# Windowed attention before a mixture of experts: token tiles handled one by one, against groups of four with 32-row score tiles and spare matmuls

## The reference

```python
qkv = layernorm(x) @ W_qkv + b_qkv                # 8 heads of 8 channels
q, k = rope2(q), rope2(k)                         # rotary, by place in an 8x8 window
attn = softmax(q * 8 ** -0.5 @ k.T + mask)        # 64 x 64 for each window and head
x = x + roll(unwindow(attn @ v)) @ W_proj + b_proj
t = layernorm(x)
gates = top2(softmax(t @ router_w.T)), normalized  # 8 experts
x = x + sum_e gates[e] * (silu(t @ w1[e].T) * (t @ w3[e].T)) @ w2[e].T   # 682 hidden
```

## Time and profile before

| | |
|---|---|
| median of 3 runs | 797.75 us (797.47 to 798.89) |
| the profiled execution's own time | 797.36 us |
| its span in the trace | 795.2 us |
| busy: PE, DVE, POOL, ACT | 688.0, 596.1, 514.5, 393.4 us |
| mean granted TensorE clock | 0.905 of full |

### The profile page before, as it was taken

The page is one execution under the profiler, slowest core; times in us unless marked ns, Lnnn a source line. Parts: engine busy times, 40 slices in busy tenths (PEclk is TensorE's granted clock), DMA queues, the critical chain, the costliest instruction groups (busy, mean ns, idle before and its releaser), DMA issues. The chain is left out here.

```text
span 795.2 us, 20947 instructions
## 1 busy us (share of the span) xinstructions
PE 688.0 (87%) x4891; PEld 449.3 (56%) x4891; DVE 596.1 (75%) x2019; ACT 393.4 (49%) x1024; POOL 514.5 (65%) x524
## 2 busy tenths in 40 slices
PE   2998898988898988898610999999999999999992
PEld 2776776766676666676410555555555555555551
DVE  4799969998999988899540577777777777777773
ACT  1455535555555555455311455555555555555551
POOL 3123666777677766665677377767677676767776
PEclk9999859898989989899655899999999999999997
DMA  9400000000000000000013244444344443444442
GB/s 340 169 8 9 22 21 13 17 19 20 20 20 20 22 19 17 20 18 24 23 27 72 39 45 46 45 46 45 44 46 45 46 45 44 45 46 45 45 45 15
DMA packets 83983, 34.17 MB, mean 43 GB/s; under 512 B 80427, under 2 KB 80876, under 8 KB 83436
## 3 DMA queue, kind: packets, MB, share of 16 engines
q0 software_dynamic: 27504, 10.10, 13.9%
q1 hardware_dynamic: 56444, 23.67, 11.6%
HBM read 20.19 MB, written 13.34 MB: 42 GB/s over the span
## 5 line engine op out<-in xcount | busy, mean ns | idle before, releaser
L1071 POOL DMA_INDIRECT out<-y_out,token x159 | 248.1, 1560 | 111.5 <-DVE y_out L955 77.1
L1011 POOL DMA_INDIRECT expert_rows<-rows,slot_u x144 | 147.8, 1026 | 55.2 <-issue 35.4
L502 PE MATMUL bank<-xs,w_sb 64*128 64x384 f32 x510 | 179.9, 497 | 1.4 <-ACT xs L630 0.8
L503 PE MATMUL bank<-xs,w_sb 64*128 64x384 f32 x510 | 180.2, 497 | 0.0
L973 DVE TENSOR_TENSOR hid<-gate_h,bank 128x384 f32<-128x384 f32 x255 | 141.0, 554 | 39.4 <-ACT gate_h L641 22.0
L641 ACT ACTIVATE gate_h<-bank 128x384 f32<-128x384 f32 x255 | 125.4, 492 | 53.7 <-PE bank L503 53.7
L502 PEld LDWEIGHTS bank<-xs,w_sb 64*128 64x128 f32 x510 | 92.1, 188 | 84.1 <-issue 34.8
L516 PE MATMUL bank<-hid,w_sb 128*64 128x384 f32 x612 | 110.0, 494 | 0.0
L503 PEld LDWEIGHTS bank<-xs,w_sb 64*128 64x128 f32 x510 | 92.1, 188 | 0.0
L399 PE MATMUL bank<-k_bd,qkt 128*128 128x512 f32 x144 | 91.3, 722 | 0.0
L650 ACT ACTIVATE y_odd<-bank 64x384 f32<-64x384 f32 x51 | 24.9, 487 | 101.0 <-PE bank L516 101.0
(11 more groups left out here) (129 smaller groups left out, 1330.9 us busy)
## 6 DMA issues: line engine op xcount, KB each, us to landing
xin<-expert_rows SPq DMA_DIRECT2D x51, 99.0 KB
xin<-expert_rows SPq DMA_DIRECT2D x51, 96.0 KB
w_sb<-w SPq DMA_DIRECT2D x1, 3072.0 KB, 22.3
out<-y_out,token POOLq DMA_INDIRECT x159, 3.1
out<-res_all SPq DMA_DIRECT2D x18, 128.0 KB
expert_rows<-rows,slot_u POOLq DMA_INDIRECT x144
x_all<-x_win SPq DMA_DIRECT2D x1, 1664.0 KB, 8.9
res_all<-x_res SPq DMA_DIRECT2D x1, 1664.0 KB, 12.4
```

Of the source, the lines that this page charges most:

```text
L502: pe.matmul(ps_h[c % RING], w13_sb[0:C, e, c, :], xs[0:C, :], start=True, stop=True)
L503: pe.matmul(ps_g[c % RING], w13_sb[C:2 * C, e, c, :], xs[C:2 * C, :], start=True, stop=True).then_inc(s_h, 1)
L1011: pool.indirect_dma_start(rows_dram, bass.IndirectOffsetOnAxis(ap=slot_u[:, i // 2, i % 2:i % 2 + 1], axis=0), rows[:, i // 2, i % 2, :], ...
L1071: pool.indirect_dma_start(out, bass.IndirectOffsetOnAxis(ap=token[:, c:c + 1], axis=0), y_out[:, c, :], None, compute_op=ALU.add).then_inc ...
```

## The change

The attention is now done group by group.

- **Projections are transposed.** ACT writes the normalized tile twice side by side (`xn[P, G, 2, C]`), so that the turned group `xt` holds the same 64 channels in rows 0 to 63 and 64 to 127. Two matmuls with 64 rows and 512 columns give q and k of the whole group, already with channels in rows and with the twin channels beside them. The rotation is one DVE instruction each for q and k (`rotate`), a third matmul with `sum_twins` adds the twins of k, and two ACT copies with a scale by row (`parity`) make `k_bd`. `rope`, `qk_bd`, the turning of q and k, and DVE's `k_bd` are gone.
- **Scores are 32-row tiles.** For a group 64 matmuls of 32 rows, 64 stationary columns and 128 moving columns take the place of four matmuls of 128x512.
- **Work by group.** The turning of `xn` and `att`, the projection, the division, and the residual addition are made for four tiles at once. v is made by 16 matmuls of 64x64.
- **Scaling moves.** Both norms' scaling goes from POOL to ACT (`normalize1`, `normalize2`, four instructions each).
- **Spare matmuls.** `turn_probs` issues two bf16 matmuls of 512 columns ahead of the turning of the last tile's probabilities and six ahead of the first tile's, into `ps_pt`, the bank that the turning overwrites. Nothing reads them.
- The bias of v is folded into that of the projection once.

```diff
+            def head_rows(pair_no, part, fresh):
+                for k in range(2):
+                    for x in range(2):
+                        heads = slice((2 * part + x) * 32, (2 * part + x + 1) * 32)
                         for w in range(2):
+                            toks = slice((2 * pair_no + k) * P + w * N, (2 * pair_no + k) * P + (w + 1) * N)
+                            at = (2 * k + part) * P
+                            mm = pe.matmul(ps[2 * pair_no + x][w * N:(w + 1) * N, at:at + P],
+                                           q_st[heads, toks], k_bd[heads, :, toks], start=fresh, stop=fresh or (part, k) == (1, 1))
...
+            def turn_probs(t, jt, spare=0):
+                after(pe, s_ptc, t, 1)
+                hold(pe)
+                for _ in range(spare):
+                    pe.matmul(ps_pt, ident_b, mask_b.unsqueeze(1).to_broadcast([P, HEADS, N]), start=True, stop=True)
+                after(pe, s_exp, t, 0)
+                hold(pe)
...
+                if ok(att_g):
+                    scores(att_g, 0, masked)
+                if ok(b - LAG_PT):
+                    turn_probs(b - LAG_PT, 3, 0 if early else 2)
+                if ok(att_g):
+                    scores_rest(att_g, 0, masked)
...
+                    turn_probs(att_g, 0, 0 if early else 6)
...
+                    scores(att_g, 1, masked)
+                    turn_probs(att_g + 1, 1)
+                    scores_rest(att_g, 1, masked)
...
+                    pe.matmul(ps_q, wqkv_sb[0:C, W_QK:W_QK + P], xt[0:C, :], start=True, stop=True)
+                    pe.matmul(ps_k, wqkv_sb[C:2 * C, W_QK:W_QK + P], xt[C:2 * C, :], start=True, stop=True).then_inc(s_qk, G)
...
+                    pe.matmul(ps_sum, sum_twins, k_st[:], start=True, stop=True).then_inc(s_sum, G)
...
+                for g in range(G):
+                    mm = act.activation(xn2[:, g, :], ln2_c[:, g, :], ACT.Copy, scale=ln2_rstd[:, g:g + 1])
+                mm.then_inc(s2xn, G)
...
+                    after(act, s_topd, route, -(G - 1))
+                    after(act, s_z, route, 1)
+                    after(act, s_gates, route, 1)
+                    act.activation(top_e[:], top_d[:], ACT.Exp).then_inc(s_tope, G)
+                if ok(b):
+                    after(act, s_sum, b, -(G - 1))
+                    after(act, s_score, b - G, -(G - 1))
+                    for k in range(2):
+                        mm = act.activation(k_bd[:, k, :], ps_sum, ACT.Copy, scale=parity[:, k:k + 1])
...
+                dve.scalar_tensor_tensor(out=dst[:].rearrange("p (w n) -> p w n", n=N), in0=src.rearrange("p (w n) -> p w n", n=N),
+                                         scalar=wqkv_sb[:, W_BIAS + which:W_BIAS + which + 1],
+                                         in1=table.unsqueeze(1).to_broadcast([P, 2 * G, N]), op0=ALU.add, op1=ALU.mult).then_inc(s_done, G)
```

More of the change, by code:

```diff
@@ new lines, in weigh_values @@
+            def weigh_values(t, jt):
+                after(pe, s_ptc, t, 0)
+                after(pe, s_vbd, t - jt, -(G - 1))
+                if jt == 0:
+                    after(pe, s_att, t - G, -(G - 1))
+                hold(pe)
+                for pr in range(4):
+                    for w in range(2):
+                        mm = pe.matmul(ps_pv[w * N:(w + 1) * N, jt * 72 + pr * 18:jt * 72 + (pr + 1) * 18],
+                                       pt[:, jt % 2, pr % 2 * 2 + pr // 2, w * N:(w + 1) * N],
+                                       v_bd[:, jt, w, pr, :], start=True, stop=True)
+                mm.then_inc(s_pv, 1)
@@ new lines, in body @@
+                if ok(route):
+                    after(pe, s_x2tc, route, -(G - 1))
+                    after(pe, s_sub, att_g + 1, 0)
+                    hold(pe)
+                    for m in range(2):
+                        mm = pe.matmul(ps_log[:, m * 2 * E:(m + 1) * 2 * E], xn2_t[:, m, :], router_sb[:], start=True, stop=True)
+                    mm.then_inc(s_log, G)
+                if ok(out_g):
+                    after(pe, s_otc, out_g, -(G - 1))
+                    after(pe, s_sub, att_g + 1, 0)
+                    hold(pe)
+                    for g in range(G):
+                        mm = pe.matmul(ps_proj[:, g * C:(g + 1) * C], att_t[:, g * P:(g + 1) * P], wproj_sb[:], start=True, stop=True)
+                    mm.then_inc(s_proj, G)
@@ new lines, in body @@
+                if ok(att_g):
+                    turn_probs(att_g + 2, 2)
+                if ok(b):
+                    after(pe, s_kst, b, -(G - 1))
+                    after(pe, s_qst, b, -(G - 1))
+                    hold(pe)
+                    pe.matmul(ps_sum, sum_twins, k_st[:], start=True, stop=True).then_inc(s_sum, G)
+                    for w in range(2 * G):
+                        for half in range(2):
+                            own = slice(half * C, (half + 1) * C)
+                            mm = pe.matmul(ps_v[own, w * C:(w + 1) * C], xt[own, w * N:(w + 1) * N], wqkv_sb[own, W_V:W_V + C], start=True, stop=True)
+                    mm.then_inc(s_v, G)
@@ L473, in _ @@
+                if ok(att_g):
+                    weigh_values(att_g + 2, 2)
             groups(pe, body)
@@ L601, in body @@
[L601 to L622 removed]
+            act.wait_ge(init_s, 2)
@@ L891, in body @@
                     dve.wait_ge(res_in, 16)
-                for j in range(G):
-                    step(b, j, ok)
+                if isinstance(b, int) and b == G:
+                    dve.wait_ge(s_bias, 1)
+                    dve.tensor_tensor(wproj_sb[C:C + 1, :], ps_bias, wproj_sb[C:C + 1, :], ALU.add).then_inc(s_biased, 1)
+                if ok(new):
+                    ln1_total(new)
+                if ok(route):
+                    ln2_squares(route)
+                if ok(new):
+                    ln1_average(new)
@@ L1165 @@
     router[C:2 * C, E:2 * E] = np.asarray(L0_ffn_router_w).T
+    wq, bq = np.asarray(L0_conv_W_qkv), np.asarray(L0_conv_b_qkv)
+    twins = np.array([p // (2 * HD) * HD + (p % HD ^ (HD // 4 if p // HD % 2 else 0)) for p in range(P)])
+    w_qkv = np.zeros((P, W_COLS), np.float32)
+    for which in range(2):
+        own = slice(which * C, (which + 1) * C)
+        w_qkv[own, W_QK:W_QK + P] = wq[:, which * C + twins]
+        w_qkv[own, W_V:W_V + C] = wq[:, 2 * C:]
+        w_qkv[:, W_BIAS + which] = bq[which * C + twins]
+    w_qkv[0:C, W_VBIAS] = bq[2 * C:]
     kf, kb, tok_id, pad = constants()
```

626 lines of the change are left out of this document (281 added, 345 removed).

## The result

The changed kernel takes **771.93 us** (median of four runs, 768.43 to 773.01); the kernel before took 797.61 beside it. The ratio is **0.967**, with a 95% interval of 0.964 to 0.971. That is a chip of what I call the first kind. In a later set of runs on a chip of that kind (whether it was the same chip is not on record) the ratio was 0.972 (0.969 to 0.976). On three further chips, the second kind, the kernel before itself took 832 us. On the one of them on which the changed kernel ran unaltered, it was 1.7% slower than the kernel before (medians 848.62 and 831.66, ratio 1.017, 1.010 to 1.024).

A forecast was written before the change was run, and what follows sets the result against it. DVE and PE were taken to bind together before the change. Gains of 15.6 us in the loops and 11 in the fill, none in the drain, take 797.4 to 770.8 us, named 771; forecast 755 to 780, with rivals 742 to 793.

The forecast's parts named there:

- The chain through a body: Loops: dependent steps through DVE, POOL, ACT, PE and the rotations set a body at 19.1 us at full clock.
- POOL not waiting for DVE: Loops, sign against the mechanism: POOL waiting for DVE by microseconds in a body would prove it wrong.
- The clock term: Loops: PE at its lower clock level 20% of the time adds 0.7 us a body; granted clock 0.88 to 0.93.
- The loops: Twelve looped bodies at 19.8 us instead of 21.1 gain 15.6 us.
- The fill: Five bodies before the loops: walked to end at 83, plus 2 for the lower clock, a gain of 11 us.
- The small matmuls side by side: Scores on PE: eight small matmuls run side by side, 0.75 us a burst, four bursts a group.
- The rival with bursts of 1.7: Scores on PE: small tiles don't run side by side, 21.2 us a body, 780 to 794 us; chance 0.15.
- its case by the rule of the Trainium skill: PE: each tiling switch exposes about 0.2 us, eight on the chain, 1.6 us a body more; within the 0.15 chance.
- Rotations: DVE: two rotations of 128x512 a group, priced at 0.685 us each, 1.4 us together.
- busy below 65% of the loops: Sign in the profile after: DVE busy below 65% of the loops; above 80% would prove the mechanism wrong.
- Spares cost nothing while exponentials are late: PE: the six end about 1 us before their exponential; uncovered they are 1.3 us, at the lower clock 2.6.
- Drain and b = 68: The written-out body and the drain: no gain; walks of the drain before and after both give 65 us.

The follow-up runs named there:

- the one that never fell: Changed kernel with all scatters ahead of the second centering, spares from the second body on, and looped bodies written out: 827.31 us, ratio 0.998.
- sixteen: Changed kernel with sixteen spare matmuls a body instead of eight: 781.68 us, 7.6 more than with eight.
- the trace with `k_bd` ahead: Changed kernel with the two k_bd copies on ACT moved ahead of the exponential of the gates: 851.6 us against 848.62.
- The written-out kernel: Changed kernel with its twelve looped bodies written out: 774.82 us; with scatters ahead and spares from the second body on as well: 827.31 us.

## Why the prediction was right, and where it was not

The sum was -26.6 and the profiled execution gave -24.3. This account is of the first kind of chip; on the second the same forecast would have been wrong, in size and in sign. Point by point:

- **The chain through a body** (19.1 at full clock): right. 18.8 in the rows above, and the undisturbed bodies of that trace start 18.2 to 18.9 us apart. By steps: DVE 1.8 for 2.35, POOL 6.1 for 6.3, ACT 4.95 for 5.4, PE with its handoffs 4.0 for 3.65, rotations 1.4; and 0.5 that the walk did not have, ACT's copy of xt ahead of normalize2, late by the two spares. No run on this kind takes a part of the chain away, so that the chain sets the body rests on these rows and their waits. The order of waits is as named: root stands right behind the scatter that ends at 213.24, normalize2 waits for it or for the xt copy, and PE's turning waits for the exponential.
- **POOL not waiting for DVE.** I wrote that a wait of POOL for DVE by microseconds in a body would prove the mechanism wrong. POOL's centering does wait: 27.4 us in twelve bodies, in the row below. The test was badly put. A chain of 19.1 with 17.7 us of POOL work in it must leave POOL idle at its entry. What the mechanism needs is no wait ahead of root, and there is none.

Waits of the changed kernel in the loops (in total, times, longest):

```profile
POOL ln_c L1056 <- DVE ln_mean L766: 27.4, 12, 5.3
...
PE bank L409 <- ACT probs L630: 11.0, 20, 1.1
```

- **The clock term** (+0.7, clock 0.88 to 0.93): right here (on the second set of runs, 0.87 and some 1.4). The mean of 19.3 less 18.6, the middle of the undisturbed bodies, is 0.7, the clock 0.90. The falls come where I looked for them: PE busy 2.63 of 4 us, and two windows later it is at 0.50. But the second pair of rows shows the same share with no fall behind it.

```profile
136.00:140.00 4.00, 2.63 (x43) 2.18 (x44) 2.11 (x6) 3.75 (x10) 2.34 (x6) 1.00 0.03 8
144.00:148.00 4.00, 4.00 (x26) 2.17 (x22) 2.85 (x17) 0.60 (x1) 0.96 (x1) 0.50 0.05 17
...
272.00:276.00 4.00, 2.64 (x31) 1.79 (x30) 3.27 (x11) 4.00 (x13) 2.27 (x6) 1.00 0.00 0
276.00:280.00 4.00, 4.00 (x53) 3.00 (x54) 1.38 (x2) 1.74 (x5) 3.16 (x5) 1.00 0.09 25
```

- **The loops** (+15.6): too low for the first runs, +21.3 (body 19.3 for 19.8), and too high for the later ones, +13.3 (20.0). The shortest bodies are alike in the two (18.2 and 18.5), so what lies between them is how often the clock fell.
- **The fill** (+11, from 95.5 - 85 = 10.5): the step that failed. "A walk of the five bodies (8, 12.6, 14.5, 17.5, 19, from 11.5) ends at 83." Measured are 14.4, 14.4, 17.7, 18.9 and 19.4, from 8.2, ending at 92.9. The first body ends 3.1 later than walked, the second adds 1.8, the third 3.2, the fourth 1.4, the fifth 0.4, 9.9 in all, and I had set aside +2 for the clock. That allowance is the term that was too small. In the first body PE's chain from the turning of `xn` to v runs at the lower level, as the twins' sum shows beside a later one at full clock; L446, q and k, L516 and L520 together last 3.1 more there than at full clock (an estimate from these and the like rows).

```profile
18.08 2.04 PE L516 MATMUL bank<-k_st,consts 128*128 128x512 f32 x2 [1.67 <-DVE k_st L866]
...
52.51 1.10 PE L516 MATMUL bank<-k_st,consts 128*128 128x512 f32 x2 [0.50 <-DVE k_st L866]
```

  The second body fell to the lower level at about 26 and took 14.4, where the one that never fell took 11.3: 3.1 more. The third takes its first 2.8 us at the lower level, 17.7 against 16.5 in that other kernel: 1.2. So the clock cost some 7.4 us for the 2 set aside (an estimate, with a trace of the second kind as the measure of full clock). Against full clock the walk itself was 1.3 too long in the second body and 2.0, 1.4 and 0.4 too short in the later ones. Which of its steps, I did not take apart.
- **The two errors cancel**: 8.4 too much in the fill, 5.7 too little in the loops (and 0.4 between the two in drain and experts). That the 771 named met 771.9 is in part luck. The body's length is what the prediction understood; the last digit, and that it was measured on a chip of the first kind, it owes to chance.
- **The small matmuls side by side**: right, 0.67 a burst against 0.75 named. The rival with bursts of 1.7 is out. So is its case by the rule of the Trainium skill, "TensorEngine Tiling (Array Packing)", key properties (a change of tiling mode drains TensorE), as a cost: from v's product to the 32-row burst (L421 to L389) starts are 0.58 apart for a product of 0.65, and from the burst to the router's full-size ones 0.59. If switching drains the array, the price lies within these figures and not on top.
- **Rotations** at 0.685 took 0.75 and 0.74; **DVE** busy below 65% of the loops: 66%, just missed. **Spares cost nothing while exponentials are late**: so for the six, which end at 216.30 in the body shown, just as the exponential does (216.35) and not 1 us ahead. Not for the two, which hold the late turning up by 0.44 there, and not for sixteen.
- **Drain and b = 68** at 0: +1.6. **Experts** carried over: 1.2 longer.

## What to carry to other kernels

When no engine is full any more, walk the chain through one body at full clock and add a term for TensorE's clock; the walk was within 2% here. Give the fill a walk of its own, body by body, with the clock's state at each, instead of scaling a loop's. And time such a change on more than one chip: a restructuring that leaves TensorE waiting in each body won 3% on one kind of chip and lost 1.7% on another, though at full clock the main instructions of each engine lasted as long on both. None of the versions here was shown to be faster than the kernel before on both kinds: with all scatters ahead the change breaks even on the second kind (ratios 0.998 to 1.004), and on the first kind that order was not run.

## What the runs showed of the hardware that I had not expected

- **Chips differ, in the attention stage alone.** The kernel before took 796 to 798 us in the first result and on one chip later, and 832 on three others. Instructions last the same: 0.624 and 0.623 us for the exponential L630, 0.988 and 0.989 for a scatter. Each chip was timed at one time only, so whether the kind belongs to the chip, or to what went on beside it then, no run here tells. In the last trace the final scatter is issued at 458.0 and lands some 2.2 later, so the experts took 363.3 us there, the 362 to 364 of the first chip. The fill is alike as well.
- **Holes in TensorE.** On the second kind PE stands still before L389 in nearly every looped body of the changed order, for 0.4 to 2.3 us, and no event of the program ends it; below are the row of the waits for the kernel with scatters ahead and early spares, looped, and the first hole of the changed kernel. On the first kind the longest such wait in the loops is 0.5.

```profile
PE bank L389 <- remote: 20.7, 10, 2.1
```

```profile
83.37 0.85 PE L389 MATMUL bank<-k_bd,q_st 32*64 32x128 f32 x16 [0.81 <-remote]
```

  The first of them over 0.4 us comes 83 to 108 us into the execution, in four of the seven traces already in the last body of the fill. They are there with loops and written out, with spares and without (shorter and more of them without). In the trace with `k_bd` ahead one shows from inside: the four transposes of a turning come one at a time.

```profile
262.50 0.27 PE L409 MATMUL bank<-consts,probs 128*128 128x128 f32 x1
263.07 0.30 PE L409 MATMUL bank<-consts,probs 128*128 128x128 f32 x1 [0.30 <-issue]
264.48 0.38 PE L409 MATMUL bank<-consts,probs 128*128 128x128 f32 x2 [1.11 <-issue]
```

  The Trainium skill, "Runtime: NRT & Kernel Launch", section on instruction fetch mechanics, says that a taken branch out of the fetched window stalls the engine. The written-out kernel has no branch in these bodies and has the holes, so that rule isn't their cause here. What is stays open: late instructions from straight fetching, or TensorE held back from outside, would both fit, and no run here tells them apart.
- **The clock's row can be wrong in the fill.** The written-out kernel's windows grant 1.00 from 29 to 36 us, where the L389 burst at 29.84 takes 1.13, its duration at the lower level. There the matmuls' own durations are to be believed.

```profile
29.00:36.00 7.00, 7.00 (x73) 4.42 (x73) 2.19 (x4) 1.47 (x3) 0.14 (x1) 1.00 0.01 2
```

- **Clock and hole feed each other, as I read it.** After a hole PE is often at the lower level (the burst at 264.26 takes 1.13 for 0.67), which lengthens the body. A body of some 24.7 us for 19.3 is more than one or two holes of 2 us; the remainder would be the clock. This is argued from the rows, not shown by a run.
